# One launch of a two-layer decoder: in the relative attention the sum and the maximum are fused per head, and three steps are put earlier

## The reference, cut to what matters

```python
q, k, val = heads(x @ Wq + bq), heads(x @ Wk + bk), heads(x @ Wv + bv)     # x is layer-normed
pos = (_sinusoid_pos_emb(S, D) @ Wp + bp).reshape(S, H, P).transpose(1, 0, 2)
content_score = jnp.einsum('bhsp,bhtp->bhst', q + u, k)
pos_score = _relative_shift(jnp.einsum('bhsp,htp->bhst', q + v, pos))
score = (content_score + pos_score) / jnp.sqrt(jnp.float32(P))
weights = jax.nn.softmax(score, axis=-1)
out = jnp.einsum('bhst,bhtp->bhsp', weights, val)
return out.transpose(0, 2, 1, 3).reshape(B, S, D) @ Wo + bo     # added to x
```

## Time and profile before

| | |
|---|---|
| median of three runs | 1761.23 us |
| profiled execution: time, span | 1756.16 us, 1754.4 us |
| first and last addition of scores (L1209) | 988.7 us, 1362.7 us |
| PE, DVE, ACT, POOL busy over the whole span | 77%, 62%, 50%, 36% |
| instructions of L1209, L1213, L1217 | 128 each, mean 685, 686, 694 ns |

### The profile page before, as it was taken

One profiled execution on the slowest core, in us unless ns is written; L12 is line 12 of the kernel. 1 busy time (PEld: TensorE's weight loads), 2 busy tenths in 40 slices (PEclk: granted clock), 3 DMA queues, 4 the chain that ended last, 5 costly groups with the idle time before them and its releaser, 6 DMA issues. The chain is left out here.

```text
span 1754.4 us, 41711 instructions
## 1 busy us (share of the span) xinstructions
PE 1351.7 (77%) x12665; PEld 858.3 (49%) x12727; DVE 1081.5 (62%) x3090; ACT 884.4 (50%) x1709; POOL 623.4 (36%) x901
## 2 busy tenths in 40 slices
PE   2687877878588888886666587887888494998998
PEld 0344444444355555554553355555555293554454
DVE  2466666665366666664543588888888614677674
ACT  1365666666366666664332476666666222322321
POOL 4365565563122222220000266666663221121110
PEclk9999999999699999998997699999999555999999
DMA  4000000000000000000000466666667100000000
GB/s 139 1 2 1 0 0 0 0 0 1 1 2 2 0 0 0 0 0 1 1 0 0 131 168 172 188 168 172 186 169 193 39 1 0 7 7 7 12 6 13
DMA packets 147215, 78.49 MB, mean 45 GB/s; under 512 B 6674, under 2 KB 146067, under 8 KB 147011
## 3 DMA queue, kind: packets, MB, share of 16 engines
q1 hardware_dynamic: 146610, 75.45, 15.8%
q0 software_dynamic: 528, 2.10, 0.4%
HBM read 41.62 MB, written 35.91 MB: 44 GB/s over the span
## 5 line engine op out<-in xcount | busy, mean ns | idle before, releaser
L715 POOL TENSOR_TENSOR rr<-ms_eps,minus_half 128x16 f32<-128x16 f32 x64 | 187.5, 2932 | 81.7 <-DVE ms_eps L927 81.7
L469 PE MATMUL psum<-identb,stacks 128*128 128x128 bf16 x1800 | 145.5, 226 | 83.0 <-DVE stacks L462 55.0
L1049 DVE TENSOR_REDUCE rowmax<-psum 128x4 f32<-128x768 f32 x128 | 122.6, 958 | 110.9 <-PE psum L1944 110.8
L469 PEld LDWEIGHTS psum<-identb,stacks 128*128 128x128 bf16 x1800 | 108.2, 101 | 129.8 <-DVE stacks L462 73.5
L966 DVE TENSOR_REDUCE rowmax<-psum 128x4 f32<-128x512 f32 x128 | 88.1, 688 | 111.7 <-PE psum L1823 111.7
L560 PE MATMUL psum<-probsT,values 128*32 128x128 f32 x2048 | 109.9, 286 | 44.0 <-DVE attn L586 43.3
L511 POOL TENSOR_TENSOR rstd<-vareps,minus_half 128x1 f32<-128x1 f32 x96 | 54.9, 572 | 176.8 <-DVE vareps L411 176.0
L1768 ACT ACTIVATE pos_rows<-psum 128x512 f32<-128x512 f32 x72 | 43.0, 597 | 128.9 <-PE psum L2280 123.2
L476 ACT ACTIVATE qT<-psum 128x1024 bf16<-128x1024 bf16 x96 | 98.8, 1029 | 5.6 <-PE psum L469 5.6
L1646 ACT ACTIVATE probsT<-psum 128x512 f32<-128x512 f32 x128 | 77.8, 608 | 44.3 <-PE psum L2149 44.3
L436 POOL CAST stacks<-staged 128x384 bf16<-128x384 f32 x87 | 59.1, 679 | 101.8 <-PE psum L469 53.9
(11 more groups left out here) (243 smaller groups left out, 3469.2 us busy)
## 6 DMA issues: line engine op xcount, KB each, us to landing
skew<-pos_rows SPq DMA_DIRECT2D x128, 258.0 KB, 4.2
pos_score<-skew SPq DMA_DIRECT2D x128, 256.0 KB, 4.3
X<-in_x_dram POOLq DMA_DIRECT2D x1, 2048.0 KB, 12.1
ctxT<-in_ctx_dram SPq DMA_DIRECT2D x1, 2048.0 KB, 10.8
out_dram<-X SPq DMA_DIRECT2D x8, 256.0 KB, 2.3
w_up<-in_L_ffn_w_e_dram SPq DMA_DIRECT2D x2, 512.0 KB, 4.0
w_down<-in_L_ffn_w_e_dram SPq DMA_DIRECT2D x2, 256.0 KB, 5.7
consts<-in_consts_dram SPq DMA_DIRECT2D x1, 401.0 KB, 3.3
```

Of the source, the lines that this page charges most:

```text
L469: last = pe.transpose(turned[:, t, :], stacks[:, which, 2 * t:2 * t + 2, :].rearrange("s h k -> s (h k)"), identb[:, :])
L715: pool.tensor_tensor(out=rr[:, par, i * H:(i + 1) * H], in0=ms_eps[:, i * H:(i + 1) * H], in1=minus_half[:, 0:H], op=ALU.pow).then_inc(A.r ...
L1049: dve.tensor_reduce(rowmax[:, par, first:first + 2 * PT - 1:2].rearrange("s (b h) -> s b h", b=2), B.max_space, AX.X, ALU.max, negate=True ...
```

## The change

DVE: each round's one addition and one maximum become four `tensor_tensor_reduce`, one per head, each of which adds a tile of 128 x 128 and also gives the row maximum; the semaphore `P.mx` is gone, and `take_max` waits for `P.add`, which the last of the four raises. In the body `normalise` moves ahead of `add_max` round 2, staging of the queries goes behind `take_max` round 2, `take_max` round 3 goes ahead of `ln_stats`, `residual_y` goes behind `add_max` of the next batch's round 0, and `ln_apply` goes to the very end. PE: `turn_out` goes ahead of `score` round 2, `turn_q2` ahead of `project` and of `turn_less` round 1, and `output` ahead of `position_score` round 1.

```diff
@@ DVE
                     wait(dve, P.pT_ps, n * R + r - 1)
-                    dve.tensor_tensor(summed[:, r % 2, :, :], P.score_bank[r % 2],
-                                      pos_score[:, par, r * PT:(r + 1) * PT, :], ALU.add).then_inc(P.add, 1)
+                    wait(dve, P.less, n * R + r - 1)
+                    dve.sem_inc(k0.carry, 1)
+                    for p in range(PT):
+                        last = dve.tensor_tensor_reduce(summed[:, r % 2, p, :], P.score_bank[r % 2][:, p, :], pos_score[:, par, r * PT + p, :],
+                                                        1.0, -3.0e38, ALU.add, ALU.max, topmost[:, r % 2, p:p + 1])
+                    last.then_inc(P.add, 1)
+
+                def take_max(n, r):
                     wait(dve, P.add, n * R + r + 1)
-                    wait(dve, P.less, n * R + r - 1)
-                    dve.tensor_reduce(topmost[:, r % 2, :], summed[:, r % 2, :, :], AX.X, ALU.max).then_inc(P.mx, 1)
-
-                def take_max(n, r):
-                    wait(dve, P.mx, n * R + r + 1)
                     dve.tensor_tensor(summed[:, r % 2, :, :], summed[:, r % 2, :, :],
                                       topmost[:, r % 2, :].unsqueeze(2).broadcast_to([S, PT, S]), ALU.subtract).then_inc(P.less, 1)
 
                 def body(b, par, left):
                     later = not isinstance(b, int) or b > 0
                     take_max(b, 1)
+                    if later:
+                        normalise(dve, P, b - 1)
+                    add_max(b, par, 2)
+                    take_max(b, 2)
                     if left >= 3:
                         stage_query(b + 3, Q2)
                         stage_query(b + 3, Q)
-                    add_max(b, par, 2)
-                    if later:
-                        normalise(dve, P, b - 1)
-                    take_max(b, 2)
-                    if left >= 3:
                         stage_key_value(b + 3, 1 - par)
                     add_max(b, par, 3)
+                    take_max(b, 3)
                     if left >= 4:
                         ln_stats(dve, P, b + 4, b + 4)
-                    take_max(b, 3)
+                    if left >= 1:
+                        add_max(b + 1, 1 - par, 0)
                     if later:
                         residual_y(dve, P, b - 1)
                     if left >= 1:
-                        add_max(b + 1, 1 - par, 0)
+                        take_max(b + 1, 0)
+                        add_max(b + 1, 1 - par, 1)
                     if left >= 4:
                         ln_apply(dve, P, b + 4, b + 4)
-                    if left >= 1:
-                        take_max(b + 1, 0)
-                        add_max(b + 1, 1 - par, 1)
@@ PE
                     turn_less(b, 0)
+                    if later:
+                        turn_out(pe, P, b - 1)
                     score(b, par, 2)
+                    if left >= 2:
+                        turn_q2(b + 2)
                     if left >= 3:
                         project(b + 3)
-                    if later:
-                        turn_out(pe, P, b - 1)
                     turn_less(b, 1)
                     score(b, par, 3)
                     weigh_values(pe, P, b, par, 0)
-                    if left >= 2:
-                        turn_q2(b + 2)
                     turn_less(b, 2)
...
                         score(b + 1, 1 - par, 0)
+                    if later:
+                        output(pe, P, b - 1, w_o1[:, :])
                     if left >= 2:
                         position_score(b + 2, 1)
-                    if later:
-                        output(pe, P, b - 1, w_o1[:, :])
                     turn_less(b, 3)
```

More of the change, by code:

```diff
@@ L305, in decoder @@
         [P.proj, P.q2, P.q, P.k, P.split, P.vst, P.v, P.bias, P.q2T_ps, P.q2T, P.qT_ps, P.qT, P.kT_ps, P.kT,
-         P.e, P.es, P.s, P.add, P.mx, P.less, P.p, P.pT_ps, P.o, P.on, P.aT_ps, P.aT,
+         P.e, P.es, P.s, P.add, P.less, P.p, P.pT_ps, P.o, P.on, P.aT_ps, P.aT,
          P.y, P.x, P.bqs, P.zeroed, P.pos] = sems(
-            "d", "proj q2 q k split vst v bias q2T_ps q2T qT_ps qT kT_ps kT e es s add mx less p pT_ps o "
+            "d", "proj q2 q k split vst v bias q2T_ps q2T qT_ps qT kT_ps kT e es s add less p pT_ps o "
             "on aT_ps aT y x bqs zeroed pos")
```

## The result

| | before | changed |
|---|---|---|
| median | 1758.62 us (4 runs, 1753.72 to 1767.03) | 1794.23 us (4 runs, 1790.48 to 1803.47) |
| ratio, 95% interval | 1 | 1.0205 [1.0146, 1.0264] |
| span of the profiled run | 1754.4 us | 1788.7 us |
| 25 periods of the stage, mean | 11.97 us (reciprocal at 1031.52 to 1330.88) | 13.35 us (1029.84 to 1363.49) |

The change makes the kernel 2% slower. The whole loss is in the relative attention: its last reciprocal starts 34.2 us later than before (1402.28 against 1368.06), and the spans differ by 34.3. The 25 periods of the table alone make 25 x 1.37 = 34.3.

What follows compares the result with a forecast made beforehand. No engine is full; a ring of waits sets the period. The new ring, 12.19 against 11.94 us, gives 28 x 0.25 = +7, tail -2: +5 on 1756.2, 1761, by the median 1766; range 1738 to 1800.

Steps and rivals of the forecast that it cites:

- Rival 1: The fused operation on DVE is dearer: at 0.35 us each 1786 us, chance 0.22; at 0.43 about 1828, chance 0.08.
- the waits: Wait before `residual_y` gone; new ones before the reciprocal (1.5 to 2), round 1's additions, `save_xnT` and `exps_turned` 1.
- the period of 12.0 to 12.3: Sign that the forecast is right: one steady period of the relative attention takes 12.0 to 12.3 us, against 11.94 before.
- The next ring: Late `ln_apply` on DVE, then `turn_xn`, `save_xnT`, `save_outT` and `turn_out`, now in series before `normalise`: a path of 2.63 us.
- T: DVE time of one fused addition and maximum, 16 per period: 0.27 us forecast, 0.43 kept for the range.
- Ring two: Ring through ACT and PE that sets the period: 11.11 us plus four fused operations, 12.19 at 0.27 each.
- Its PE term: PE before `turn_less` 1: `turn_out`, `score` and `project` together 1.51 us, and `turn_q2`, new in front, 0.56.
- the forecast's small term for the last four bodies: Nothing is projected there and DVE binds: 4 x 4 x (1.42 - 1.08 - 0.12), a gain of some 3 us, 2 counted.
- nothing overlaps: Fused operations on DVE cost full durations, 0.43 us each: period 14.11, about 1828 us in all; chance 0.08.
- Rival 2: DVE's own 9.77 us sets the period: about 1700 us, or 1730 if one ring opens in part; chance 0.17.

Runs made afterwards that it cites:

- e3: The changed kernel with `ln_apply` one place earlier on DVE, ahead of `add_max` of the next batch's round 1: 1730.54 us, ratio 0.9855.
- e4: The changed kernel with seven extra, unused transposes on PE just before the wait for `turn_xn`: 1757.90 us, ratio 0.9993.
- e1: The kernel before with only the fusion, the bodies of DVE and PE left in their old order: 1743.61 us, ratio 0.9917.
- e2: The changed kernel's order on DVE and PE, with the unfused addition and maximum: 1804.57 us, ratio 1.0264 to the kernel before.
- e7: As e3, but with the unfused addition and maximum: 1736.51 us, ratio 0.9867 to the kernel before.
- e13: The kernel before with three extra, unused transposes on PE, where it has no long wait for `turn_xn`: 1770.19 us, ratio 1.0065.

## Why the prediction was right and where it failed

The forecast was "no change", 1766 us; the kernel is slower, ratio 1.0205 [1.0146, 1.0264]. 1794 lies in the range, near the 1786 of the first rival, but not by that rival's mechanism. The range reached up to 1800 for the sake of a dearer operation, and the operation came out cheaper; that it holds the measured time is luck. Of the signs named in advance, the waits came true and the period of 12.0 to 12.3 did not.

- **The next ring: right, and shown.** That `ln_apply` at the end puts `turn_xn`, `save_xnT`, `save_outT` and `turn_out` in series with `normalise` is what e3 opens. The wait before the reciprocal was forecast at about 1.7; it is 1.41 and 1.71 in turn at full clock (e4). The wait before round 1's additions was put at 0.6; with the smaller T it is 0.70 and 0.94 there. On ACT, `save_xnT` waits 0.73 and `exps_turned` 1 waits 2.25, as forecast.
- **T: too large.** 0.27 forecast, 0.21 measured. I had added the one-column write in full; its row starts with the next fused operation, and it costs next to nothing. Ring two with 0.85 for the four is 11.11 + 0.85 = 11.96; e4 measured 12.08. So the sum was right to 1% in a kernel whose clock holds, and not by luck: followed link by link through one period of e4, no link differs from its term by more than 0.15. Its PE term, `turn_out` to `turn_less` round 1, 1.51 + 0.56 = 2.07, is 2.07 in e4. (In the forecast's small term for the last four bodies, 1.42 stands in no row. The mean of the four distances is 1.35, which makes the term 2.4 instead of 3, and changes nothing.)
- **The clock: the step that failed.** The prediction took every PE step of the ring from rows at clock 1.00 and did not ask what the new wait in front of them does to the clock. That term, 2.07, is 2.90 to 3.80 in 21 of the 25 periods, and 3.20 in the mean of all. So this stretch alone makes 1.13 of the 1.26 by which the mean period, 13.35, exceeds the 12.08 of e4; the rest was not followed. 28 x 1.26 makes 35 us, and e4 gives back 36.
- **Rival 1, a dearer operation: wrong.** T is 0.21, e1 is faster than before. The price of "nothing overlaps", 0.43, is out: starts lie 0.21 apart although each operation lasts 0.28. The prediction laid that price to the Trainium skill's page "VectorE: DVE Perf Modes", section "The DRAIN you can't avoid", but the same section adds: "A next op that is not held starts earlier". The trace agrees with that, with its 0.21. The same page's section "Two Vector instructions with no wait between them" says that an operation with an accumulator output is two instructions; the trace agrees, there are 512 rows of each kind.
- **Rival 2, DVE alone sets the period: wrong** in every run. Even e3 is at 11.2, not 9.8.
- **Fusion and moves nearly add.** Alone they are -14 us (e1) and +47 (e2), which makes +33, and together they are +36; with `ln_apply` early, the moves alone give -20 (e7), with e1's -14 that makes -34, and both give -27 (e3). Neither gap is clear of the noise.

The Trainium skill's page "TensorE: Matmul & The Clock Gate", section "HAM oscillation — how this bites in real kernels", describes a kernel in which a wait in every tile lets the clock fall again and again, so that each tile starts slow. The trace agrees in that the clock falls again in most periods; here, in the 25 periods, no single wait of PE was longer than 0.89 us.

That the fallen clock costs the time is shown by e4. What makes it fall in one period and not in another stays open. The length of a wait alone does not decide: around 1016 of the changed kernel PE waits 0.91 and 0.24 and the clock holds, and in the kernel before PE stands 1.45 in every period and the clock is 1.00 from 1010 to 1350.

## What to carry to other kernels

When a move takes one wait away, write down the next ring through every in-order queue, and put the last instruction of a loop's body and the first of the next in it: an instruction that other engines need belongs into a place where its own engine waits anyway. Then ask what PE does in the waits of the new ring: if it stands just before a run of matmuls that others wait for, cost those matmuls at the lower clock as well, as a second case; a wait does not always bring it (the 1.45 of before did not). A few useless transposes in the wait are a quick test for that, and here a cure, but the order that removes the wait gave 27 us more, and in e13, at a place without a wait, they made the kernel slower.

## What the hardware showed that I had not expected

- The fused addition and maximum of 128 x 128 fp32, one source in PSUM, costs DVE 0.21 us; the read of the maximum (0.08 long) starts together with the next operation. A plain operation of this size costs 0.20. So a round, added and with its maxima, takes 0.85 in four pieces against 1.32 in two whole passes.
- The clock of PE fell to 1.2 GHz after three short waits (0.86, 0.24, 0.25 with instructions of 0.33 and 0.65 between) and came back about 3.4 us later; in e2 and e13 it took nearly 7. In the profiled executions seven extra transposes in the longest wait kept it up in every period from 1010 to 1350, three in all but one, one in some of them only. A single wait of 1.45 in every period of the kernel before left it up.
